# Shared bias added at the routed evictions, four gathered token tiles, layernorm statistics in pieces

## The reference

```
x = x + attention0(layernorm(x), ctx)    # one head of 512; keys: 256 context tokens, 256 own
x = x + ffn0(layernorm(x))               # ternary weights, 8-bit activations, 2048 hidden
x = x + attention1(layernorm(x), ctx)    # 16 heads of 128, 4 groups, rms-normed q and k
x = x + ffn1(layernorm(x))

def ffn1(x):                             # 8 experts, best 2 for each token, and a shared one
    probs = softmax(x @ router_w.T); topk_w, topk_idx = top_k(probs, 2)
    topk_w = topk_w / sum(topk_w)        # the two weights of a token sum to 1
    moe = sum over a token's two experts e: topk_w[e] * (silu(x @ gw[e]) * (x @ uw[e])) @ dw[e]
    shared = silu(x @ s_gate_w + s_gate_b) * (x @ s_up_w + s_up_b) @ s_down_w + s_down_b
    return moe + shared
```

## Time and profile before

| | us |
|---|---|
| median of 3 runs (lowest to highest) | 1943.16 (1940.67 to 1944.83) |
| the profiled execution | 1958.19 |
| its span | 1955.6 |
| PE busy in it | 1782.2 |
| DVE busy | 1248.0 |
| ACT busy | 890.7 |
| POOL busy | 574.9 |

### The profile page before, as it was taken

The page is one execution under the profiler, slowest core; times in us unless marked ns, Lnnn a source line. Parts: engine busy times, 40 slices in busy tenths (PEclk is TensorE's granted clock), DMA queues, the critical chain, the costliest instruction groups (busy, mean ns, idle before and its releaser), DMA issues. The chain is left out here.

```text
span 1955.6 us, 27616 instructions
## 1 busy us (share of the span) xinstructions
PE 1782.2 (91%) x10202; PEld 1470.8 (75%) x10226; DVE 1248.0 (64%) x2351; ACT 890.7 (46%) x1662; POOL 574.9 (29%) x415
## 2 busy tenths in 40 slices
PE   4999997884799958999999999999887999999988
PEld 4898995673344537888888888888755789999866
DVE  5334332776888745776777767777566567676545
ACT  3233331574566634544555445555231256566311
POOL 2111011221656622121221212211042145555233
PEclk8999998897899988999999999999988999999989
DMA  5011012463001144121321212210061378888553
GB/s 215 22 32 32 21 54 75 160 227 142 1 22 44 44 136 158 55 76 55 103 96 61 76 55 79 95 65 1 0 230 43 103 256 273 281 278 267 190 188 124
DMA packets 127649, 217.00 MB, mean 111 GB/s; under 512 B 8358, under 2 KB 68006, under 8 KB 125350
## 3 DMA queue, kind: packets, MB, share of 16 engines
q1 hardware_dynamic: 117644, 181.11, 27.2%
q0 software_dynamic: 9888, 34.35, 5.7%
HBM read 171.65 MB, written 43.78 MB: 110 GB/s over the span
## 5 line engine op out<-in xcount | busy, mean ns | idle before, releaser
L1368 POOL TENSOR_TENSOR a_rq<-a_ssq,a_mhalf 128x4 f32<-128x4 f32 x64 | 65.1, 1017 | 414.1 <-DVE a_ssq L1492 414.1
L78 PE MATMUL bank<-a_xT_hi,a_wq_lo 128*128 128x512 f32 (+1 forms) x384 | 144.6, 377 | 19.0 <-PEq L56 15.0
L1453 ACT ACTIVATE a_pT_hi<-bank 128x512 fp32r<-128x512 f32 x128 | 69.5, 599 | 192.6 <-PE bank L1620 192.6
L1447 ACT ACTIVATE a_scores<-a_scores,a_nmax 128x256 f32<-128x256 f32 x256 | 127.2, 503 | 30.4 <-DVE a_nmax L1507 30.2
L79 PE MATMUL bank<-a_xT_lo,a_wq_hi 128*128 128x512 f32 (+1 forms) x384 | 139.3, 363 | 0.0
L80 PE MATMUL bank<-a_xT_hi,a_wq_hi 128*128 128x512 f32 (+1 forms) x384 | 139.1, 362 | 0.0
L78 PE MATMUL bank<-a_wo_hi,a_oT_lo 128*128 128x512 f32 x320 | 128.2, 401 | 2.7 <-DVE a_oT_lo L409 1.4
L80 PE MATMUL bank<-a_wo_hi,a_oT_hi 128*128 128x512 f32 x320 | 126.5, 395 | 0.0
L79 PE MATMUL bank<-a_wo_lo,a_oT_hi 128*128 128x512 f32 x320 | 126.4, 395 | 0.0
L1500 DVE SCALAR_TENSOR_TENSOR a_scores<-bank,a_rq,a_mask 128x256 f32<-128x256 f32 x256 | 106.2, 478 | 29.1 <-PE bank L80 20.8
L1908 POOL TENSOR_TENSOR e_wg_lo<-raw_g,e_wg_hi 128x1408 fp32r<-128x1408 f32 x26 | 91.2, 3509 | 113.0 <-ACT e_wg_hi L1981 113.0
(11 more groups left out here) (406 smaller groups left out, 5457.8 us busy)
## 6 DMA issues: line engine op xcount, KB each, us to landing
raw_g<-in_egw SPq DMA_DIRECT2D x26, 704.0 KB, 4.6
raw_u<-in_euw SPq DMA_DIRECT2D x26, 704.0 KB, 6.1
a_xT_hi<-x1T_hi SPq DMA_DIRECT2D x16, 1024.0 KB, 5.9
a_xT_lo<-x1T_lo SPq DMA_DIRECT2D x16, 1024.0 KB, 8.2
raw_d<-in_edw SPq DMA_DIRECT2D x26, 512.0 KB, 6.0
y_routed<-m_y SPq DMA_DIRECT2D x39, 256.0 KB, 6.6
raw_d<-in_edw SPq DMA_DIRECT2D x26, 192.0 KB, 6.8
a_cTraw<-in_ctxT SPq DMA_DIRECT2D x8, 512.0 KB, 3.5
```

The costliest lines, as they stand in the source:

```text
L78: pe.matmul(out, w[1], x[0], start=first, stop=False)
L1368: pool.tensor_tensor(rq[:, h % HG, :], ssq[:, h % HG, :], mhalf[:], ALU.pow).then_inc(s_rq, 1)
L1447: act.activation(row, row, ACT.Exp, bias=nmax[:, i % 2, t:t + 1], accum_out=den[:, i % 2, t:t + 1]).then_inc(s_exp, 1)
L1453: act.activation(pT[b].hi[:], ptb[b][:].rearrange("p (k s) -> p k s", k=QT), ACT.Copy).then_inc(ft.hi, 1)
```

## The change

- Attention 0: X comes in three transfers, the third (tiles 4 to 15) behind wo. The statistics of batch k are taken for that batch alone: batch 0 first, batch 1 before the queries' split, batch i+2 in turn i, between the split of the transposed tokens and the maxima. The inverse root of var + eps is POOL's power instead of ACT's square root and DVE's reciprocal. ACT copies wo before the values, PE waits for wo's low half ahead of each output projection, and DVE's first six turns are written out instead of looped.
- Attention 1: the statistics of one tile ahead of `output` in each head of the last group's chunks 1 to 3; the add of eps in the very last head.
- Feed-forward 1: no additions of `sdb` to X. `output` adds `sdb` to each routed row at its eviction (the two weights of a token sum to 1). `msg` is gone, silu and product work in `mhf`. The gathers have four pairs of buffers. POOL writes the low half of the first up weights before the power for the last four tiles.

```diff
@@ attention0, sync, gpsimd, scalar
-            sp.dma_start(X[:, QT:T, :], x_dram[:, QT:T, :]).then_inc(s_x[1], 16)
+            sp.dma_start(X[:, QT:2 * QT, :], x_dram[:, QT:2 * QT, :]).then_inc(s_x[1], 16)
...
                 sp.dma_start(wraw[j - 2][:], w_dram[j]).then_inc(s_w[j], 16)
+            sp.dma_start(X[:, 2 * QT:T, :], x_dram[:, 2 * QT:T, :]).then_inc(s_x[2], 16)
...
+            def inverse(k):
+
+                pool.wait_ge(s_ve, at(k + 1))
+                pool.tensor_tensor(rstd[:], ve[:], mhalf[:], ALU.pow).then_inc(s_rstd, 1)
...
-            with pool.Fori(1, B) as i:
+            with pool.Fori(1, B - 1) as i:
+                inverse(i + 1)
                 context(i)
+            context(B - 1)
...
             context_values(0)
+            weights(3)
             values(0)
-            weights(3)
@@ attention0, vector
+            def statistics(k):
+                for t in range(QT):
+                    dve.bn_stats(stats[:, t:t + 1, :], X[:, bass.ds(k * QT + t, 1), :]).then_inc(s_stats, 1)
+                for t in range(QT):
+                    dve.wait_ge(s_stats, at(k * QT + t + 1))
                     dve.bn_aggr(mv[:, t, :], stats[:, t, :]).then_inc(s_mv, 1)
+                dve.wait_ge(s_mv, at(k * QT + QT))
+                dve.tensor_scalar(ve[:], mv[:, :, 1], LN_EPS, None, ALU.add).then_inc(s_ve, 1)
...
                 if more:
                     transposed_x(i + 1)
+                if next_norm:
+                    statistics(i + 2)
...
             weights(1)
+            dve.wait_ge(s_x[1], at(16))
+            statistics(1)
+            queries(0)
             weights(2)
-            dve.wait_ge(s_x[1], at(16))
-            statistics(range(QT, T))
-            queries(0)
-            inverse(slice(QT, T), 2)
             norm(1)
             keys(0)
             values(0)
-            with dve.Fori(0, B - 2) as i:
+            dve.wait_ge(s_x[2], at(16))
+            for i in range(B - 2):
                 turn(i, True, True)
@@ attention0, tensor, in turn and ahead of the loop
+                pe.wait_ge(s_wolo, at(1))
                 pe.wait_ge(o.lo, at(i * 2 + 2))
...
-            pe.wait_ge(s_wolo, at(1))
@@ attention1, vector
+                if n > (G - 1) * NC:
+                    statistics(n - 1, (n % NC - 1) * CT + i % HG)
+                    if u == G * U - 1:
+                        dve.wait_ge(s_lmv, T - CT)
+                        dve.tensor_scalar(last.ve[:, 0:T - CT], last.mv[:, 0:T - CT, 1], LN_EPS, None, ALU.add).then_inc(s_lve, 1)
                 output(u, i)
@@ feed_forward1, gpsimd
-            pool.wait_ge(last.small_loaded, 64)
-            pool.wait_ge(s_xn, T)
-            for t in range(T):
-                pool.tensor_tensor(X[:, t, :], X[:, t, :], sdb[:], ALU.add).then_inc(s_bias, 1)
...
-                    if t >= 2:
-                        pool.wait_ge(s_mix, (t - 2) * TOP + n + 1)
+                    if t >= YG:
+                        pool.wait_ge(s_mix, (t - YG) * TOP + n + 1)
@@ feed_forward1, scalar and vector
-                act.wait_ge(s_h, SV + n - 1)
-                act.activation(msg[n % 2][:], gb[(SV + n) % 2][:, 0:I], ACT.Silu).then_inc(s_sg, 1)
+                after(act, ht.mm, n - 1)
+                act.activation(mhf[n % 2][:, 0:I], gb[(SV + n) % 2][:, 0:I], ACT.Silu).then_inc(s_sg, 1)
...
-                dve.tensor_copy(y[n % 3][:], yb[(T + n) % 2][:]).then_inc(s_taken, 1)
+                dve.tensor_tensor(y[n % 3][:], yb[(T + n) % 2][:], sdb[:], ALU.add).then_inc(s_taken, 1)
```

More of the change, by code:

```diff
@@ L183, in attention0 @@
         wraw = [sb(f"wraw{j}", [P, KD, D]) for j in range(2)]
[L184 to L187, removed]
+        stats = sb("stats", [P, QT, 6])
+        mv = sb("mv", [P, QT, 2])
+        ve, rstd, mhalf = (sb(n, [P, QT]) for n in ("ve", "rstd", "mhalf"))
         xn = sb("xn", [P, QT, D])
@@ L201, in attention0 @@
         bank = banks
-        s_x = [sem(f"x{j}_loaded") for j in range(2)]
+        s_x = [sem(f"x{j}_loaded") for j in range(3)]
         s_w = [sem(f"w{j}_loaded") for j in range(4)]
@@ L424, in _ @@
             dve.wait_ge(s_x[0], at(16))
-            statistics(range(QT))
-            inverse(slice(0, QT), 1)
+            statistics(0)
             norm(0)
@@ L1567, in _ @@
                     add(n, n % NC)
-                if n > (G - 1) * NC and i % HG == 1:
-                    statistics(n - 1, n % NC - 1)
-                    if n == G * NC - 1:
-                        dve.wait_ge(s_lmv, T - CT)
-                        dve.tensor_scalar(last.ve[:, 0:T - CT], last.mv[:, 0:T - CT, 1], LN_EPS, None, ALU.add).then_inc(s_lve, 1)
         @block.tensor
@@ L1746, in feed_forward1 @@
         xg = [Region(nc, xn_at + j * 4 * D).take(f"m_xg{j}", [P, D]) for j in range(XG)]
-        yg = [[Region(nc, xn_at + (2 * j + n) * 4 * D).take(f"e_yg{j}{n}", [P, D]) for n in range(TOP)] for j in range(2)]
+        YG = 4
+        yg_mem = [Region(nc, xn_at), Region(nc, small_at)]
+        yg = [[yg_mem[j // 2].take(f"e_yg{j}{n}", [P, D]) for n in range(TOP)] for j in range(YG)]
         idhot = Region(nc, y_at).take("r_idhot", [P, T * TOP, 2, NT], BF16)
@@ L1751, in feed_forward1 @@
         hT = [tile_mem.pair(f"m_hT{j}", [P, M, P]) for j in range(2)]
-        msg = [tile_mem.take(f"m_sg{j}", [P, I]) for j in range(2)]
-        mhf = [mem_of.take(f"m_hf{j}", [P, M * P]) for j, mem_of in enumerate((tile_mem, Region(nc, last.sdb_at)))]
+        mhf = [tile_mem.take(f"m_hf{j}", [P, M * P]) for j in range(2)]
         sb = lambda name, shape, dt=F32: mem.take("r_" + name, shape, dt)
@@ L2149, in routed_gated @@
                 dve.wait_ge(s_u, SV + n + 1)
-                after(dve, ht.mm, max(n - 1, 0))
-                dve.tensor_tensor(mhf[n % 2][:, 0:I], ub[(SV + n) % 2][:, 0:I], msg[n % 2][:], ALU.mult).then_inc(s_h, 1)
+                gated = mhf[n % 2][:, 0:I]
+                dve.tensor_tensor(gated, ub[(SV + n) % 2][:, 0:I], gated, ALU.mult).then_inc(s_h, 1)
             def routed_hT(n):
@@ L2172, in combine @@
                     row = X[:, t, :]
-                    dve.scalar_tensor_tensor(row, yg[t % 2][n][:], weight[:, t, n:n + 1], row, ALU.mult,
+                    dve.scalar_tensor_tensor(row, yg[t % YG][n][:], weight[:, t, n:n + 1], row, ALU.mult,
                                              ALU.add).then_inc(s_mix, 1)
@@ L2398, in _ @@
                 add(t, t)
+            dve.wait_ge(last.small_loaded, 64)
             for n in range(NT):
```

58 lines of the change are left out of this document (24 added, 34 removed).

## The result

The changed kernel takes 1912.67 us (median; 1911.22 to 1915.04), the kernel before 1942.7 us beside it: a ratio of 0.9846, 95% interval 0.9829 to 0.9864. That is 30.0 us gained where 44.5 were forecast. The direction was right; 1912.67 us lies 14 us above the forecast of 1898.7 and 0.7 us above the range.

A forecast was written before the change was run, and what follows sets the result against it. PE, busy 91% of the span, bounds the kernel, so only its waits and low clock can go. 15.8 + 2.6 + 14.9 + 11.2 = 44.5 us off the 1943.16 us median gives 1898.7 us, range 1891 to 1912 us.

The forecast's parts named there:

- a single wait of about that length: Last feed-forward: PE's 12.2 us token-split wait behind POOL's bias additions goes; with the low clock behind it, 14.9 us.
- the other terms: Start of attention 0, 15.8 us; its turns, 0; end of attention 1, 2.6 us; four gather buffer pairs in the tail, 11.2 us.
- one row contradicts a rule: Last feed-forward: r_h_lo's 14.14 us taken as held by POOL's additions, though the skill says blocking lasts one instruction.
- a wait that is made shorter: End of attention 1: a_pT_lo starts 1.2 us earlier, and 0.6 us of PE's other waits for it goes.
- clock term: End of attention 1: low clock behind PE's a_pT_lo wait costs 1.5 us; half taken, 0.8 us, between 0 and 1.5.

## What to carry to other kernels

Where the profiled execution is longer than the median, first look for a single wait of about that length, and take that wait out of the sum until a second profile shows it; the other terms can be right to a microsecond or two and the total still be off by it. When one row contradicts a rule, look through the same line's other instances for one that meets the same condition: here the second stood 99 us further on. And a wait that is made shorter but stays among other gaps may pay in clock what it gives in time, so its clock term is bounded below nothing too.

## What the runs showed of the hardware

In 690 trials a subtraction of DVE with both inputs in SBUF ended no earlier than 0.54 us behind the end of the POOL addition that it met; arrivals 2 to 3 ns apart around that end differ by one whole addition, 689 against 1815 ns. In the kernels such an instruction can lose many turns in a row to back-to-back additions: 14.14 us through eleven of them in one trace, 4.84 us through four in another, and 13 of 98 executions have a time that fits the first. With one PSUM input and one in SBUF, 39 evictions of 0.68 us showed no hold (676 to 692 ns), 23 of which began while a gate split of POOL ran.

Being held past a second POOL instruction isn't always rare. In attention 1 of all 14 traces of whole kernels, a multiplication of DVE (L1516 in before, 0.35 us by itself) that begins 0.3 us into a DMA issue of POOL's is recorded as 2.0 us, six times in each, and ends only 0.16 us behind the POOL split that follows the issue. No run here tries why:

```profile
773.08 0.82 POOL L1381 DMA_DIRECT2D ahead_raw<-in_Wq  x1 [0.31 <-POOL a_wo_lo L1378]
773.93 1.29 POOL L1385 TENSOR_TENSOR a_K_lo<-ahead_ctx,a_K_hi 128x512 fp32r<-128x512 f32 x1
```

```profile
773.37 2.02 DVE L1516 TENSOR_SCALAR a_scores<-a_scores,a_rden 128x256 f32<-128x256 f32 x1
```
